# Feed-forward with quantised weights kept as integers and the low-rank term apart

## The chip, the cores and the metric

One core of a Trainium2 chip runs the kernel. The metric is the device time of one execution in microseconds. The engines are TensorE (PE in the rows; its weight loads are PEld), VectorE (DVE), ScalarE (ACT), GpSimd (POOL) and SyncE (SP), each with its own queue that is worked off in order. A semaphore is counted up by one engine and waited for by another.

## The reference, cut to what matters

Two layers act on 16 x 256 rows of 256 numbers, each with an attention half and a feed-forward half. The change touches the feed-forward of the first layer, whose weights are rounded to 8 bits and have a low-rank addition:

```python
def fake_quant_weight(w, bits=BITS):
    qmax = 2.0 ** (bits - 1) - 1
    scale = jnp.max(jnp.abs(w)) / qmax
    wq = jnp.clip(jnp.round(w / scale), -qmax - 1, qmax) * scale
...
def qat_lora_linear(x, W, b, A, B):
    base = jnp.einsum('bsi,oi->bso', x, Wq) + b
    lora = jnp.einsum('bsr,or->bso', jnp.einsum('bsi,ri->bsr', x, A), B)
    return base + SCALING * lora
h = qat_lora_linear(hidden_states, W_fc, b_fc, A_fc, B_fc)
h = jax.nn.gelu(h, approximate=False)
h = qat_lora_linear(h, W_proj, b_proj, A_proj, B_proj)
...
x = x + jnp.tanh(g_ffn[0]) * _L0_ffn_ref(_layernorm(x, axis=-1), ...)
```

The rank is 16, SCALING is 2, W_fc is 1024 x 256 and W_proj is 256 x 1024.

## The kernel before

The kernel runs in stages, one after the other, with a barrier of all engines between them: the gates of the first attention (`mlstm_gates`, 0 to about 76 us), its heads (`mlstm_heads`, to 218), the feed-forward (`phase_lora_ffn`, to 414), the second attention (to about 790) and the routed experts with the shared ones (to the end).

Products in float32 of full precision are made of three passes of TensorE. Each operand is split into a part rounded to the fast format (hi) and a rest (lo), and `three_passes` (lines 29 to 34) adds hi x hi, hi x lo and lo x hi in PSUM.

**The gate stage.** Eight steps n each take 512 rows: DVE makes the statistics and the normalised rows `z`, PE turns them (`turn`), ACT copies them, and PE makes the gate rows (`context_part`, `query_part`). Between these steps the two weights of the feed-forward are prepared. PE multiplies the low-rank factors in 8 pieces (`delta_piece`, ahead of everything else on its queue) and ACT keeps each piece times 2 (`keep_delta`). DVE takes the largest absolute value (`largest`); PE turns the maxima of the partitions (`turn_amax`, which stands behind the pieces), DVE derives the step (`scales`), rounds (`quantise`) and adds the low-rank product (`add_delta`); ACT makes the hi part (`split_w1`, `split_w2`) and DVE the lo part (`low_part`).

**The feed-forward.** Eight chunks n each take 512 rows (T = 4 tiles of 128). The hidden layer has KF = 8 blocks m of 128 units by 512 rows, in HR = 4 PSUM banks `hid`. For each block PE issues 2 x 3 products of 512 columns. ACT then runs the gelu twice, once in float32 (`g_full`, of which there are GR = 2) and once rounded (`g_hi`), and DVE subtracts (`g_lo`). PE's `outputs(n)` makes 4 tiles x 8 blocks x 3 products of 256 columns into `y`, and it may start with the blocks below EARLY = 6. Between `hidden(n)` and `outputs(n)` PE turns the next chunk's rows (`transpose_z(n + 1)`) into two banks `zt`, which ACT and DVE split. DVE adds `y` to `x_all` (`add_x`), in two halves. The order of work on each engine is written by hand: on PE hidden, transpose, outputs; on DVE statistics and norm of the next chunk, the eight `g_lo`, the split of `zt`, `add_x`. POOL takes the power for the norm and adds the output bias.

The quoted lines are the order on PE before.

```python
            with pe.Fori(0, CHUNKS - 1) as n:
                hidden(n)
                transpose_z(n + 1)
                outputs(n)
            hidden(CHUNKS - 1)
            outputs(CHUNKS - 1)
```

## Time and profile before

| | us |
|---|---|
| median of 3 runs | 1389.59 |
| lowest, highest | 1383.13, 1390.19 |
| span of the profiled execution | 1389.1 |
| feed-forward, PE's first product to the last addition | 220.0 to 414.4 |

The profile is one execution. A page gives the busy time of each engine; further views list the instructions in order of time, the groups of instructions, the waits, and the busy time in chosen stretches. PE's products overlap: a product of 512 columns is listed with 0.40 us, while the next starts 0.233 us behind it, so its cost is the distance of starts. The granted clock of PE is given as a share of 2.4 GHz; it is 1.00 or 0.50.

### The profile page before, as it was taken

How to read it: one execution, taken by the hardware profiler on the slowest of the kernel's cores; microseconds unless marked ns; L12 is line 12 of the kernel's file. 1: busy time of each engine (PE TensorE's matmuls, PEld its weight loads, DVE VectorE, ACT ScalarE, POOL GpSimd, SP SyncE). 2: the span in 40 equal slices, each digit the busy share in tenths (PEclk: the TensorE clock that was granted, in tenths of full speed). 3: DMA queues.
4: the chain of work that ended last, by engine and by line, in shares of the span. 5: the costliest groups of instructions: out<-in, count | busy, mean ns of one | idle time of the engine just before them, and what ended most of it. 6: DMA issues, size and time to landing. Idle time of an engine off the chain costs nothing. (4 is left out here: it accounts for less than half of the span.)

```text
span 1389.1 us, 28714 instructions
## 1 busy us (share of the span) xinstructions
PE 1214.8 (87%) x9632; PEld 1021.2 (74%) x9633; DVE 875.0 (63%) x1963; ACT 713.7 (51%) x1580; POOL 425.8 (31%) x557
## 2 busy tenths in 40 slices
PE   7878887999995899999998689767899999995888
PEld 3246556989884566666666488667899999995888
DVE  4959996454535677777787266335566676662546
ACT  2478874464531466666666443124555555553343
POOL 1148876231302011111110016453033233214552
PEclk9979999999996799999999868788999999997999
DMA  8156531000006243344331056444345555534552
GB/s 287 53 206 201 198 115 46 0 0 0 0 0 109 65 99 98 79 97 100 80 87 48 13 203 217 155 170 164 123 160 165 168 161 172 164 117 171 186 190 76
DMA packets 97630, 164.71 MB, mean 119 GB/s; under 512 B 12263, under 2 KB 71835, under 8 KB 95227
## 3 DMA queue, kind: packets, MB, share of 16 engines
q1 hardware_dynamic: 87643, 136.11, 32.3%
q0 software_dynamic: 9264, 27.01, 5.9%
q8 instruction: 57, 0.93, 0.3%
q10 hardware_dynamic: 624, 0.32, 0.1%
q14 instruction: 42, 0.34, 0.1%
HBM read 103.66 MB, written 33.69 MB: 99 GB/s over the span
## 5 line engine op out<-in xcount | busy, mean ns | idle before, releaser
L1449 DVE TENSOR_REDUCE c_mx<-c_s 128x2 f32<-128x512 f32 x256 | 164.5, 685 | 73.1 <-PE c_s L1591 73.1
L1372 ACT ACTIVATE c_probs<-c_t 128x512 f32<-128x512 f32 x256 | 138.9, 595 | 8.8 <-PE c_t L1613 6.0
L2405 ACT ACTIVATE de_g_full<-de_hid,d_e_bias 128x256 f32<-128x256 f32 x156 | 77.1, 494 | 105.5 <-PE de_hid L34 105.5
L32 PE MATMUL de_hid<-de_zt_hi,d_e_hi 128*128 128x256 f32 x312 | 90.5, 290 | 1.4 <-DVE de_zt_lo L2429 1.4
L957 ACT ACTIVATE b_g_full<-b_hid,b_b 128x512 f32<-128x512 f32 x64 | 44.2, 691 | 90.1 <-PE b_hid L34 71.3
L1591 PE MATMUL c_s<-c_kt,c_qt 48*128 48x256 f32 x512 | 64.8, 332 | 26.9 <-DVE c_mx L1449 26.9
L34 PE MATMUL de_y_ps<-d_w_hi,de_g_lo 128*128 x312 | 88.2, 283 | 0.0
L32 PE MATMUL de_y_ps<-d_w_hi,de_g_hi 128*128 x312 | 88.1, 282 | 0.0
L33 PE MATMUL de_y_ps<-d_w_lo,de_g_hi 128*128 x312 | 88.0, 282 | 0.0
L34 PE MATMUL de_hid<-de_zt_hi,d_e_lo 128*128 128x256 f32 x312 | 87.1, 279 | 0.0
L33 PE MATMUL de_hid<-de_zt_lo,d_e_hi 128*128 128x256 f32 x312 | 87.1, 279 | 0.0
L1310 POOL CAST c_ct_hi<-c_c_raw 128x512 fp32r<-128x512 f32 x15 | 9.1, 609 | 243.6 <-PE c_misc L34 243.6
L2562 POOL DMA_INDIRECT dc_rows<-d_y_rows,d_pos x64 | 61.8, 966 | 69.0 <-DVE x_all L2595 32.6
L2434 DVE TENSOR_TENSOR de_g_lo<-de_g_full,de_g_hi 128x256 fp32r<-128x256 f32 x156 | 64.7, 454 | 26.5 <-ACT de_g_hi L2406 26.5
L2406 ACT ACTIVATE de_g_hi<-de_hid,d_e_bias 128x256 fp32r<-128x256 f32 x156 | 77.9, 499 | 0.0
L1591 PEld LDWEIGHTS c_s<-c_kt,c_qt 48*128 48x128 f32 x512 | 41.3, 197 | 43.9 <-DVE c_mx L1449 25.0
L32 PE MATMUL b_y<-b_w_hi,b_g_hi 128*128 128x256 f32 x256 | 72.9, 285 | 0.7 <-DVE b_g_lo L1048 0.7
L33 PE MATMUL b_y<-b_w_lo,b_g_hi 128*128 128x256 f32 x256 | 72.4, 283 | 0.0
L34 PE MATMUL b_y<-b_w_hi,b_g_lo 128*128 128x256 f32 x256 | 72.4, 283 | 0.0
L1625 PE MATMUL c_o<-c_probs,c_va 128*32 128x256 f32 x1024 | 70.7, 395 | 1.2 <-ACT c_probs L1372 1.2
L1951 POOL DMA_INDIRECT d_z_rows<-dr_z,dr_pos_i x56 | 55.6, 994 | 50.1 <-DVE dr_pos_i L2099 34.2
L1613 PEld LDWEIGHTS c_t<-c_qt,c_kt 50*128 50x128 f32 x512 | 39.8, 191 | 41.7 <-issue 24.5
(385 smaller groups left out, 4159.4 us busy)
## 6 DMA issues: line engine op xcount, KB each, us to landing
d_e_raw<-in_w SPq DMA_DIRECT2D x39, 514.0 KB, 5.4
a_mb<-a_maxima SPq DMA_DIRECT2D x16, 1024.0 KB, 7.3
d_z_in<-d_z_rows POOLq DMA_DIRECT2D x39, 256.0 KB, 3.9
d_y_rows<-de_ys SPq DMA_DIRECT2D x39, 256.0 KB
c_kt<-c_k_hi SPq DMA_DIRECT2D x64, 128.0 KB, 3.1
c_qt<-c_q_hi SPq DMA_DIRECT2D x64, 128.0 KB, 3.3
d_zt_kept<-d_w_hi SPq DMA_DIRECT2D x32, 256.0 KB
d_w_hi<-d_zt_kept SPq DMA_DIRECT2D x16, 512.0 KB, 3.7
```

The lines of the kernel that those rows point to most:

```text
L32: tensor.matmul(out, lhs_hi, rhs_hi, start=start, stop=False)
L33: tensor.matmul(out, lhs_hi, rhs_lo, start=False, stop=False)
L34: return tensor.matmul(out, lhs_lo, rhs_hi, start=False, stop=stop)
L1372: act.activation(probs[h % PR][:], t_ps[k][:], ACT.Exp).then_inc(exp_done, 1)
L1449: dve.tensor_reduce(mx[n % 2][:, :, k, p:p + 1], s_ps[h % SB][:], AX.X, ALU.max).then_inc(max_done, 1)
L1591: mm = pe.matmul(s_ps[(first + k) % SB][:, j, :], qt[u][rows, p, j * P:(j + 1) * P], kt[u][rows, p, :], start=True, stop=True)
L1625: mm = pe.matmul(o_ps[OSLOT * i:OSLOT * (i + 1), g % 2, :], va[n % R][:, j, h, :], probs[(n * H + h) % PR][:, j, :], start=(j == 0), stop= ...
L1951: pool.indirect_dma_start(z_rows, bass.IndirectOffsetOnAxis(ap=pos_i[:, at:at + 1], axis=0), z_tile(i), None).then_inc(scattered[2 * i // ...
L2405: act.activation(g_full[:, m, :], hid[m][:, 0:TOK], ACT.Gelu, bias=bias[u][:, m:m + 1]).then_inc(gelu_full, 1)
L2406: act.activation(g_hi[u][:, m, :], hid[m][:, 0:TOK], ACT.Gelu, bias=bias[u][:, m:m + 1]).then_inc(gelu_hi, 1)
L2434: dve.tensor_tensor(g_lo[u][:, m, :], g_full[:, m, :], g_hi[u][:, m, :], ALU.subtract).then_inc(gelu_lo, 1)
L2562: pool.indirect_dma_start(rows[n % RR][:, t * TOP + k, :], None, y_rows, bass.IndirectOffsetOnAxis(ap=M.pos[:, T * n + t, k:k + 1], axis=0 ...
```

## The change

The quantised weight is a step size times an integer of at most 8 bits. After the change the weights `w1` and `w2` hold the integers themselves, which the fast format holds whole, so their lo part is zero and is left out: a product of weight and activation takes two passes (hi and lo of the activation). The step size is applied after the sum: as ACT's `scale` in the gelu (a tensor, one value per partition) and as DVE's scalar in `add_x`.

The low-rank term is no longer multiplied out. For the first layer PE lowers the rows to the rank with `down` (`lower(n)`, 4 products of 512 columns), ACT rounds the result into `low`, DVE puts the lo part beside it, and one further product per block (`raised(m)`) adds the term to `hid`. For the second layer `w2` is 32 columns wider (288), so that `outputs` also gives the lowered rows; DVE copies them (`keep_low2`), PE turns them (`turn_low2`), ACT rounds, DVE makes the lo part (`split_low2`), and 4 products of 256 columns add the term to `y` (`close`). These last steps of chunk n stand inside `hidden(n + 1)`. The up factors are divided by the step size in the gate stage (`raise_hi`, `raise_lo`).

PSUM is dealt out anew: HR = 3 banks `hid`, one bank `turned` for both halves of `zt` and both lowered results, four banks `y`. EARLY is 5. In the gate stage `delta_piece`, `keep_delta`, both `add_delta` and the four splits of the weights are gone, and two new loads (`lora_down`, `lora_up`, 0.57 MB) take the place of four (0.16 MB).

```diff
+        self.G = 2 * rank
+        self.WIDE = self.D + self.G
+        self.w1, self.w2 = sb("w1", [P, self.KD, self.FF]), sb("w2", [P, self.KF, self.WIDE])
+        self.down, self.up = sb("down", [P, self.KD, P]), sb("up", [P, self.FF + self.D])
...
-            act.wait_ge(tanh_done, 1)
-            act.activation(tanh_2[:], tanh_g[:, 2:3], ACT.Copy, scale=2.0).then_inc(tanh_done, 1)
-
-            def keep_delta(k):
-                i, q = divmod(k, PIECES)
-                act.wait_ge(delta_done, k + 1)
-                if k == PIECES:
-                    act.wait_ge(tanh_done, 2)
-                act.activation(delta[i][:, PIECE * q:PIECE * (q + 1)], delta_ps[k % 2], ACT.Identity,
-                               scale=2.0 if i == 0 else tanh_2[:]).then_inc(delta_kept, 1)
...
+            def raise_hi(i):
+                cols = slice(0, lora.FF) if i == 0 else slice(lora.FF, lora.FF + D)
+                act.wait_ge(inverted, i + 1)
+                act.activation(lora.up[0:3 * G, cols], up_raw[:, cols], ACT.Identity, scale=inv2[0:3 * G, i:i + 1]).then_inc(up_hi_done, 1)
...
             def quantise(i):
                 flat = w_raw[i][:]
+                kept = lora.w1[:].rearrange("p a b -> p (a b)") if i == 0 else lora.w2[:, :, 0:D]
                 chained(dve.tensor_scalar(flat, flat, inv[:, i:i + 1], ROUND, ALU.mult, ALU.add))
                 chained(dve.tensor_scalar(flat, flat, -ROUND, QMAX, ALU.add, ALU.min))
-                chained(dve.tensor_scalar(flat, flat, -QMAX - 1.0, scale[:, i:i + 1], ALU.max, ALU.mult))
-
-            def add_delta():
-                flat = w_raw[0][:]
-                dve.wait_ge(delta_kept, PIECES)
...
-            def delta_piece(k):
-                i, q = divmod(k, PIECES)
-                after(pe, delta_kept, k - 1)
...
-                pe.wait_ge(delta_kept, 2 * PIECES)
...
-    HR = 4
+    HR = 3
     GR = 2
-    EARLY = 6
+    EARLY = 5
...
+            def round_low2(n):
+                act.wait_ge(low2_turned, n + 1)
+                act.activation(low2[:], turned[:], ACT.Copy).then_inc(low2_hi_done, 1)
+
+            def gelu(n, m):
+                act.wait_ge(hid_done, n * KF + m + 1)
+                act.wait_ge(gelu_lo, n * KF + m + 1)
+                act.activation(g_full[:, m % GR, :], hid[m % HR][:], ACT.Gelu,
+                               bias=b1[:, m:m + 1], scale=lora.scale[:, 0:1]).then_inc(gelu_full, 1)
+                act.activation(g_hi[:, m, :], hid[m % HR][:], ACT.Gelu,
+                               bias=b1[:, m:m + 1], scale=lora.scale[:, 0:1]).then_inc(gelu_hi, 1)
+
+            round_low(0)
+            for m in range(KF):
+                gelu(0, m)
+            with act.Fori(0, CHUNKS - 1) as n:
+                split_zt(n + 1)
+                round_low(n + 1)
                 for m in range(KF):
-                    act.wait_ge(hid_done, n * KF + m + 1)
-                    act.wait_ge(gelu_lo, n * KF + m + 1)
-                    act.activation(g_full[:, m % GR, :], hid[m % HR][:], ACT.Gelu,
-                                   bias=b1[:, m:m + 1]).then_inc(gelu_full, 1)
-                    act.activation(g_hi[:, m, :], hid[m % HR][:], ACT.Gelu,
-                                   bias=b1[:, m:m + 1]).then_inc(gelu_hi, 1)
-
-            with act.Fori(0, CHUNKS - 1) as n:
-                gelus(n)
-                split_zt(n + 1)
-            gelus(CHUNKS - 1)
+                    gelu(n + 1, m)
+                    if m == 2:
+                        round_low2(n)
...
+            def split_low(n):
+                dve.wait_ge(low_hi_done, n + 1)
+                dve.tensor_tensor(low[pair, :], turned[pair, :], low[pair, :], ALU.subtract).then_inc(low_lo_done, 1)
+
+            def keep_low2(n):
+                for t in range(T):
+                    dve.wait_ge(sums_done, n * T + t + 1)
+                    dve.tensor_copy(low2_rows[:, t, 0:3 * G].rearrange("p (k g) -> p k g", k=3),
+                                    y[t][:, D:WIDE].rearrange("p (k g) -> p k g", k=1).broadcast_to([P, 3, G])).then_inc(low2_kept, 1)
+
+            def split_low2(n):
+                dve.wait_ge(low2_hi_done, n + 1)
+                dve.tensor_tensor(low2[pair, :], turned[pair, :], low2[pair, :], ALU.subtract).then_inc(low2_lo_done, 1)
+
+            def split_gelu(n, m):
+                dve.wait_ge(gelu_hi, n * KF + m + 1)
+                dve.wait_ge(gelu_full, n * KF + m + 1)
+                dve.tensor_tensor(g_lo[:, m, :], g_full[:, m % GR, :], g_hi[:, m, :],
+                                  ALU.subtract).then_inc(gelu_lo, 1)
+
+            def add_x(n, t):
+                dve.wait_ge(y_done, n * T + t + 1)
+                dve.wait_ge(x_biased, n * T + T)
+                xs = x_all[:, n * T + t, :]
+                dve.scalar_tensor_tensor(out=xs, in0=y[t][:, 0:D], scalar=lora.scale[:, 1:2], in1=xs,
+                                         op0=ALU.mult, op1=ALU.add).then_inc(x_added, 1)
...
+            def between(n, more):
                 split_zt(n + 1)
-                add_x(n)
-
+                if more:
+                    stat(n + 2)
+                else:
+                    dve.wait_ge(w_loaded, 64)
+                    dve.tensor_scalar(w_raw[:, :, 3 * D:], w_raw[:, :, 3 * D:], tanh_g[:, 1:2], None, ALU.mult).then_inc(wc_scaled, 1)
+                split_low(n + 1)
+                keep_low2(n)
+                if more:
+                    norm(n + 2)
+                for m in range(KF):
+                    split_gelu(n + 1, m)
+                    if m == 3:
+                        split_low2(n)
+                    if m >= T:
+                        add_x(n, m - T)
...
+            def lower(n):
+                pe.wait_ge(zt_lo_done, n * KD + KD)
                 for c in range(KD):
-                    for t in range(T):
-                        mm = pe.transpose(zt[c][:, t * P:(t + 1) * P], z[:, t, c * P:(c + 1) * P], ident[:])
-                    mm.then_inc(zt_done, 1)
-
-            def hidden(n):
-                pe.wait_ge(zt_lo_done, n * KD + KD)
+                    for part in (zt_hi, zt_lo):
+                        mm = pe.matmul(turned[:], down[:, c, :], part[:, c, :], start=(c == 0 and part is zt_hi), stop=(c == KD - 1 and part is zt_lo))
+                mm.then_inc(low_done, 1)
+
+            def base(n, m):
+                if m >= HR:
+                    pe.wait_ge(gelu_hi, n * KF + m + 1 - HR)
+                for c in range(KD):
+                    for part in (zt_hi, zt_lo):
+                        pe.matmul(hid[m % HR][:], w1[:, c, m * P:(m + 1) * P], part[:, c, :], start=(c == 0 and part is zt_hi), stop=False)
+
+            def raised(m):
+                pe.matmul(hid[m % HR][:], up[:, m * P:(m + 1) * P], low[:], start=False, stop=True).then_inc(hid_done, 1)
...
+            def hidden(n, tail):
                 for m in range(KF):
-                    pe.wait_ge(gelu_hi, n * KF + m + 1)
-                    cols = slice(m * P, (m + 1) * P)
-                    for c in range(KD):
-                        mm = three_passes(pe, hid[m % HR][:], (w1_hi[:, c, cols], w1_lo[:, c, cols]),
-                                          (zt_hi[:, c, :], zt_lo[:, c, :]), c == 0, c == KD - 1)
-                    mm.then_inc(hid_done, 1)
-
-            def outputs(n):
-                def product(t, m):
-                    cols = slice(t * P, (t + 1) * P)
-                    return three_passes(pe, y[t // 2][:, t % 2, :], (g_hi[:, m, cols], g_lo[:, m, cols]),
-                                        (w2_hi[:, m, :], w2_lo[:, m, :]), m == 0, m == KF - 1)
-
-
-                pe.wait_ge(x_added, n * (T // 2))
+                    base(n, m)
+                    if m == 0:
+                        pe.wait_ge(low_lo_done, n + 1)
+                    raised(m)
+                    if tail and m == 1:
+                        turn_low2(n - 1)
+                    if tail and m == 3:
+                        close(n - 1)
...
+            def product(t, m):
+                cols = slice(t * P, (t + 1) * P)
+                pe.matmul(y[t][:, 0:WIDE], g_hi[:, m, cols], w2[:, m, :], start=(m == 0), stop=False)
+                return pe.matmul(y[t][:, 0:WIDE], g_lo[:, m, cols], w2[:, m, :], start=False, stop=(m == KF - 1))
...
+            def outputs(n, more):
+                if more:
+                    transpose_z(n + 1, 0)
                 pe.wait_ge(gelu_lo, GR + n * KF + EARLY)
-                for t in range(0, T, 2):
+                for t in range(T):
                     for m in range(EARLY):
                         product(t, m)
+                if more:
+                    transpose_z(n + 1, 1)
                 pe.wait_ge(gelu_lo, GR + n * KF + KF)
                 for t in range(T):
-                    for m in range(0 if t % 2 else EARLY, KF):
+                    for m in range(EARLY, KF):
                         mm = product(t, m)
-                    if t % 2:
-                        mm.then_inc(y_done, 1)
-
+                    mm.then_inc(sums_done, 1)
+                    if more and t == 1:
+                        lower(n + 1)
...
+            def turn_low2(n):
+                pe.wait_ge(low2_kept, n * T + T)
+                for t in range(T):
+                    mm = pe.transpose(turned[:, t * P:(t + 1) * P], low2_rows[:, t, :], ident[:])
+                mm.then_inc(low2_turned, 1)
+
+            def close(n):
+                pe.wait_ge(low2_lo_done, n + 1)
+                for t in range(T):
+                    pe.matmul(y[t][:, 0:D], low2[:, t * P:(t + 1) * P], up[:, FF:FF + D], start=False, stop=True,
+                              skip_group_check=True).then_inc(y_done, 1)
+
+            lower(0)
+            hidden_first()
             with pe.Fori(0, CHUNKS - 1) as n:
-                hidden(n)
-                transpose_z(n + 1)
-                outputs(n)
-            hidden(CHUNKS - 1)
-            outputs(CHUNKS - 1)
+                outputs(n, True)
+                hidden(n + 1, True)
+                pe.wait_ge(x_added, n * T + T)
```

On PE, where block 3 of the hidden layer ends and block 4 begins, before (the names in brackets are semaphores, whose names are used again from an earlier stage; here the one that counts rounded gelus):

```order
L34 MATMUL b_hid3<-b_zt_hi,b_w1_lo 128x512
L32 MATMUL b_hid3<-b_zt_hi,b_w1_hi 128x512
L33 MATMUL b_hid3<-b_zt_lo,b_w1_hi 128x512
L34 MATMUL b_hid3<-b_zt_hi,b_w1_lo 128x512
L1127 REGISTER_ALU
L32 MATMUL b_hid0<-b_zt_hi,b_w1_hi 128x512 [waits ag_ready]
```

The same place after, inside the loop (`ag_x_loaded5` counts DVE's `split_low2`, `ag_kt_loaded0` the rounded gelus):

```order
L1151 MATMUL b_hid0<-b_zt_lo,b_w1 128x512
L1154 MATMUL b_hid0<-b_low,b_up 128x512
L1208 MATMUL b_y0<-b_up,b_low2 128x256 [waits ag_x_loaded5]
L1208 MATMUL b_y1<-b_up,b_low2 128x256
L1208 MATMUL b_y2<-b_up,b_low2 128x256
L1208 MATMUL b_y3<-b_up,b_low2 128x256
L1148 REGISTER_ALU
L1151 MATMUL b_hid1<-b_zt_hi,b_w1 128x512 [waits ag_kt_loaded0]
```

The closing products of the chunk before stand between the two blocks, and the first of them waits for DVE.

On DVE at that place after (blocks 2 to 4 of the gelu; `ag_x_loaded4` counts ACT's rounding of `low2`, the other two the gelus):

```order
L1048 TENSOR_TENSOR b_g_lo<-b_g_full,b_g_hi 128x512 [waits ag_x_loaded7,ag_kt_loaded0]
L1046 REGISTER_ALU
L1048 TENSOR_TENSOR b_g_lo<-b_g_full,b_g_hi 128x512 [waits ag_x_loaded7,ag_kt_loaded0]
L1043 TENSOR_TENSOR b_low2<-b_turned,b_low2 32x512 [waits ag_x_loaded4]
L1046 REGISTER_ALU
L1048 TENSOR_TENSOR b_g_lo<-b_g_full,b_g_hi 128x512 [waits ag_x_loaded7,ag_kt_loaded0]
L1055 ISA [waits ag_w_loaded0,ag_kt_loaded2]
L1055 SCALAR_TENSOR_TENSOR x_all<-b_y0,b_scale,x_all 128x256
```

`split_low2` stands behind the low part of gelu 3, and the first addition to `x_all` behind that of gelu 4; before, eight low parts stood in a row there and the additions behind them and the split of `zt`.

On PE at the end of the loop's body after (`ag_kt_loaded3` counts the additions to `x_all`):

```order
L1151 MATMUL b_hid1<-b_zt_lo,b_w1 128x512
L1154 MATMUL b_hid1<-b_low,b_up 128x512
L1213 REGISTER_ALU [waits ag_kt_loaded3]
L1213 COMPARE_AND_BRANCH
L1179 MATMUL b_y0<-b_w2,b_g_hi 128x288 [waits ag_kt_loaded1]
```

Before, the wait for the additions stood at the head of `outputs`, behind the hidden layer, and was for the additions of the chunk before; now a wait for those of the chunk that the body began with stands behind the next chunk's hidden layer.

## Rows read from the trace of the kernel before

**Rows 1.** The page: span, and busy time, share and instructions of the engines.
```profile
span 1389.1 us, 28714 instructions
PE 1214.8 (87%) x9632; PEld 1021.2 (74%) x9633; DVE 875.0 (63%) x1963; ACT 713.7 (51%) x1580; POOL 425.8 (31%) x557
```

**Rows 2.** Busy time by stretch, one in the feed-forward; last PEclk, DMA share, GB/s.
```profile
265.00:290.00 25.00, 25.00 (x165) 22.72 (x165) 11.72 (x24) 11.94 (x19) 5.87 (x6) 1.00 0.00 0
```

**Rows 3.** Waits of PE from 237 to 413.9: total us, times, longest.
```profile
PE b_y L32 <- DVE b_g_lo L1048: 0.7, 1, 0.7
```

**Rows 4.** Groups of instructions, 205 to 415: busy us, mean ns, idle before.
```profile
L1048 DVE TENSOR_TENSOR b_g_lo<-b_g_full,b_g_hi 128x512 fp32r<-128x512 f32 x64 | 49.6, 785 | 23.3 <-ACT b_g_hi L959 23.2
...
L957 ACT ACTIVATE b_g_full<-b_hid,b_b 128x512 f32<-128x512 f32 x64 | 44.2, 691 | 90.1 <-PE b_hid L34 71.3 <-DVE b_g_lo L1048 16.9
L959 ACT ACTIVATE b_g_hi<-b_hid,b_b 128x512 fp32r<-128x512 f32 x64 | 44.0, 687 | 0.0
```

**Rows 5.** PE in order of time, one chunk: start us, length us, instruction.
```profile
249.04 0.40 PE L32 MATMUL b_hid<-b_zt_hi,b_w_hi 128*128 128x512 f32 x1
...
260.24 1.03 PE L1121 MATMUL b_zt<-ident,b_z 128*128 128x128 f32 x8
261.03 0.36 PE L32 MATMUL b_y<-b_w_hi,b_g_hi 128*128 128x256 f32 x1
...
272.63 0.40 PE L32 MATMUL b_hid<-b_zt_hi,b_w_hi 128*128 128x512 f32 x1
```

**Rows 6.** PE, ACT and DVE in order of time, last block of the last chunk.
```profile
401.80 0.39 PE L34 MATMUL b_hid<-b_zt_hi,b_w_lo 128*128 128x512 f32 x1
...
402.23 0.69 ACT L957 ACTIVATE b_g_full<-b_hid,b_b 128x512 f32<-128x512 f32 x1
402.82 0.68 ACT L959 ACTIVATE b_g_hi<-b_hid,b_b 128x512 fp32r<-128x512 f32 x1
...
403.53 0.69 DVE L1048 TENSOR_TENSOR b_g_lo<-b_g_full,b_g_hi 128x512 fp32r<-128x512 f32 x1 [0.71 <-ACT b_g_hi L959]
```

**Rows 7.** PE and DVE in order of time, start and end of the stage.
```profile
220.04 0.79 PE L32 MATMUL b_hid<-b_zt_hi,b_w_hi 128*128 128x512 f32 x1 [4.27 <-DVEq L1062]
...
237.46 0.35 PE L32 MATMUL b_y<-b_w_hi,b_g_hi 128*128 128x256 f32 x1 [0.66 <-DVE b_g_lo L1048]
...
229.46 1.38 DVE L1036 TENSOR_SCALAR b_z<-x_all,b_mean_var,b_rstd 128x256 f32<-128x256 f32 x4 [3.20 <-POOL b_rstd L978]
...
413.75 0.69 DVE L1056 TENSOR_TENSOR x_all<-x_all,b_y 128x512 f32<-128x512 f32 x1 [2.91 <-PE b_y L34]
```

**Rows 8.** PE after three idle times, and stretches behind them as in rows 2.
```profile
36.97 1.11 PE L519 MATMUL ag_tz<-ident,ag_z 128*128 128x128 f32 x8 [3.59 <-DVE ag_z L402]
...
232.85 0.50 PE L32 MATMUL b_hid<-b_zt_hi,b_w_hi 128*128 128x512 f32 x1 [1.61 <-ACT b_g_hi L959]
...
416.23 0.66 PE L1549 MATMUL c_misc<-ident,c_z 128*128 128x128 f32 x4 [2.52 <-DVEq L1492]
...
416.80:420.20 3.40, 3.40 (x18) 3.40 (x18) 0.81 (x2) 1.20 (x2) 1.80 (x3) 0.50 0.18 29
...
38.00:41.30 3.30, 3.30 (x5) 0.78 (x5) 3.16 (x11) 0.75 (x2) 0.23 (x1) 0.50 0.00 0
...
230.50:236.00 5.50, 3.89 (x19) 2.81 (x18) 4.35 (x7) 4.46 (x8) 5.08 (x5) 1.00 0.00 0
```

**Rows 9.** PE, DVE and ACT in order of time, gate stage.
```profile
18.46 1.91 PE L509 MATMUL ag_tok<-ag_factors 16*128 16x256 f32 x4
...
13.37 1.41 DVE L390 BATCH_NORM_STATS2 ag_stats<-x_all 128x6 f32<-128x256 f32 x4 [5.16 <-DMA x_all<-in_x]
...
28.99 0.29 DVE L413 TENSOR_REDUCE ag_amax<-ag_spare 128x1 f32<-128x128 f32 x1 [6.70 <-PE ag_spare L526]
...
14.17 0.60 ACT L334 ACTIVATE ag_delta<-ag_tok 128x512 f32<-128x512 f32 x1 [1.11 <-PE ag_tok L506]
15.29 0.69 ACT L334 ACTIVATE b_delta<-ag_spare,ag_tanh 128x512 f32<-128x512 f32 x1 [0.52 <-PE ag_spare L509]
```

More of the change, by code:

```diff
@@ L934, in phase_lora_ffn @@
         block = ctx.enter_context(nc.Block())
+        pair = slice(G, 2 * G)
         @block.sync
@@ L945, in _ @@
         def _(act):
-            act.sem_inc(gelu_hi, HR)
             def split_zt(n):
@@ L1051, in add_x @@
[L1051 to L1062 removed]
+                    dve.tensor_tensor(zt_lo[:, c, :], turned[:], zt_hi[:, c, :], ALU.subtract).then_inc(zt_lo_done, 1)
@@ L1086, in _ @@
             norm(1)
-            split_gelu(0)
-            split_zt(1)
-            add_x(0)
+            for m in range(KF):
+                split_gelu(0, m)
             dve.wait_ge(h_x_done, HT)
-            with dve.Fori(1, CHUNKS - 1) as n:
-                step(n)
-            dve.wait_ge(w_loaded, 64)
-            dve.tensor_scalar(w_raw[:, :, 3 * D:], w_raw[:, :, 3 * D:], tanh_g[:, 1:2], None, ALU.mult).then_inc(wc_scaled, 1)
-            split_gelu(CHUNKS - 1)
-            dve.wait_ge(x_added, T // 2)
+            dve.wait_ge(padded, 1)
+            with dve.Fori(0, CHUNKS - 2) as n:
+                between(n, True)
+            between(CHUNKS - 2, False)
+            dve.wait_ge(x_added, T)
             for j in range(attn.J):
@@ L1162 @@
+            outputs(CHUNKS - 1, False)
+            turn_low2(CHUNKS - 1)
+            close(CHUNKS - 1)
 class RoutedRows:
```

213 lines of the change are left out of this document (101 added, 112 removed).

## Prediction

> **What bounds the kernel now.** I read the page first: TensorE (PE) is busy for 87% of the span [rows 1]. The change touches two of five stages: the gate stage (0 to 76 us) and the feed-forward (220 to 414 us). So next the busy time by stretch: in a 25 us stretch of the feed-forward PE is busy for all of it at full granted clock, ScalarE (ACT) and VectorE (DVE) for half [rows 2]. Then the waits of PE alone: from 237 us to the end of the stage it waits once, 0.7 us [rows 3]. The feed-forward is bound by PE's issue rate, and the other two have slack. The reader is to see that this slack is an average: within a chunk each gelu pair (1.15 us of ACT per 512-column block) hangs on PE's last product and DVE's low part hangs on the gelu [rows 4, 6].
>
> **Part 1, work taken off PE.** One chunk before: 48 products of 512 columns in 249.04 to 260.24 (11.20 us, 0.2333 each), 8 transposes in 0.79 (0.099 each), 96 products of 256 columns in 11.60 (0.1208 each), together 23.59 us [rows 5]. After, a chunk has 40 products of 512 columns for the hidden layer and 4 for the lowered rank (44 x 0.2333 = 10.27), 64 of 288 columns, 12 transposes (1.19) and 4 closing products of 256 columns (0.48). No row shows 288 columns; it lies between 0.1208 and 0.2333. I take the straight line between the two, 0.135, since it is nearest to 256 columns: 8.63. Sum 20.57, so 3.0 us less per chunk. At 0.1208 the saving would be 3.9, at 0.2333 a loss of 3.3. The Trainium skill ("TensorE: Matmul & The Clock Gate", section "Back-to-back issue gap") gives N/2.4 + 2.5 ns for one product, 122.5 ns at 288 columns; as an estimate by that page the chunk would be 0.8 us shorter still, 6 us over eight chunks, but its 215.8 ns at 512 columns is below the 233 ns of rows 5, so the trace decides.
>
> **Part 2, two new waits, which PE has nothing to cover with.** Before, PE waits in the hidden layer only for a bank that was read four blocks ago, and between chunks only for sums that were added long before. After, the second layer's low-rank term is closed inside the next chunk's hidden layer.
>
> Wait A: behind block 3 PE issues `close`, which needs DVE's low part of `low2`. On DVE that instruction stands behind the low part of gelu 3, and gelu 3 needs the block that PE has just issued. So PE waits for the whole ladder PE, ACT, ACT, DVE, DVE. Rows 6 show this ladder at the end of a chunk: the block's last product starts at 401.80, the gelus at 402.23 and 402.82, DVE's low part ends at 403.53 + 0.69 = 404.22. From PE's next free slot (402.03) that is 2.19 us. To it come DVE's `low2` part, 0.65 more (a 512-column subtraction of the same kind), and 0.53 because ACT rounds `low2` just ahead of gelu 3: 3.4 us. Behind the waiting instruction on PE are `close` and blocks 4 to 7, and ACT and DVE wait for these.
>
> Wait B: at the loop's end PE waits for `x_added`. The fourth `add_x` stands on DVE behind the low part of gelu 7, so the same ladder runs again: 2.19 + about 0.4 for a 256-column add = 2.6 us. Behind it are the next chunk's transposes and all its output products, though those need only gelus 0 to 4.
>
> Each wait also costs 0.1 for the restart (the product after the gap at 232.85 takes 0.50 [rows 8], others 0.40). Together 6.2 us per chunk in seven chunks, against 3.0 saved: a period of 23.59 becomes 26.7. The range of A is 2.2 (its ACT and DVE parts hidden) to 4; of B 2.2 to 3.
>
> **Part 3, the two ends of the stage.** First chunk: PE starts at 220.04 [rows 7]. Now 4 lowering products come first, at half clock as before at this place (the first one takes 0.79 [rows 7] and not 0.40 [rows 5]; spaced by 0.45), and DVE's first instruction waits for ACT's rounding of them: 1.8 + 0.6 + 0.7 + 0.2 = 3.3 us before its statistics start. These lead to the normalised rows at 229.46, behind which the first gelu low part stands; it goes to 232.8. ACT then needs three gelu pairs more for the five blocks, and PE's output products begin near 239.1 (before 237.46). With 8.6 of products, 0.4 of transposes and 0.9 of lowering, the second chunk starts at 249.1, as before (249.04 [rows 5]). So the first chunk gains nothing. Periods 1 to 6: 6 x 3.15 = +18.9. Last chunk: before, from 390.6 (249.04 + 6 x 23.59) to 414.44 [rows 7], 23.9 us. After: hidden layer 9.3 + 0.9 of turning and closing + 6.2 of waits + 8.6 of products = 25.0, then a tail that nothing covers (copy, 4 transposes, ACT's rounding 0.6, DVE's part 0.7, closing, four adds): about 4.3. Sum 29.3, +5.4. Stage: +24.3 us.
>
> **Part 4, the clock.** A PE idle of 2.52 us is followed by a stretch at 0.50 of the granted clock (1.2 GHz in place of 2.4) from 416.8 to 420.2; one of 3.59 us by one from 38 to 41.3; one of 1.61 us leaves it at 1.00 [rows 8]. The new waits are 3.4 and 2.6 us, so most should be followed by such a stretch. It halves 3.4 us of work, which PE must then make up: 1.7 us, in stretches that PE bounds (blocks 4 to 7 after A, output products after B). Fourteen waits give 0 to 24 us; since B stands at the edge of what rows 8 show, I count ten: +17. The Trainium skill ("TensorE: Matmul & The Clock Gate", section "Loop structure matters more than you think") says the same of a loop whose every pass waits between bursts, namely that each burst then runs cold; rows 8 bear that out for single gaps, and no run here shows it for a loop.
>
> **Part 5, the gate stage.** Sixteen groups of small products and their ACT copies go, and so do DVE's two sums and two low parts. PE was at them until 20.4 us, which kept the turned maxima from DVE: it sat idle 6.70 us until 28.99 [rows 9]. Then came PE's idle of 3.59 us until 36.97 [rows 8], and from there PE is the chain to the stage's end. After, DVE's second statistics start at 13.37 [rows 9] plus about 1 us, since the new factor table adds 0.4 MB to what loads then. Statistics, normalising and maxima put the first turn on PE near 18, and with two half-clock groups behind it the maxima near 24.5; DVE goes on near 24.8 in place of 28.99, and the third turn falls near 32.6, not 36.97: -4 us, an estimate from these rows. DVE's work at the stage's end gets shorter too, but there the last rows' placing is later, so that is hidden. Bounds: -8 (all of DVE's gain) to 0 (a further cold stretch).
>
> **Part 6, a second per-partition operand in the gelu.** ACT's copy with a tensor as scale took 0.69, with a number 0.60 [rows 9]. The gelu already has a tensor bias at 0.69 [rows 4]. If a second tensor costs again, every ladder grows by up to 0.3: 0 to 5 us, taken as 2.
>
> **The sum.** 24.3 + 17 - 4 + 2 = +39 us on the profiled execution's 1389.1, hence 1428. The median of the three runs is 1389.6, 0.5 from it, so no correction. Attention and the experts are untouched.
>
> **Rivals.** (1) The waits come but the clock stays up: gaps of 2.6 and 3.4 us inside dense work need not behave like those of rows 8. Then 1389 + 24 - 4 + 0 to 2 = 1409 to 1411. For it: the gap of 1.61 us. Against: that of 2.52. 15 in 100.
> (2) Faster: the two waits are covered. The place is PE's queue behind block 3 and block 7. It decides at 3.0 us of wait per chunk; below it the change wins. If ACT and DVE ran ahead so that both vanish, 7 x 3.0 and the gate stage's 4 give 1364. Against it: the ladder of rows 6 has 2.19 us in it twice, whatever the order of the rest, and the program leaves PE no other instruction there. 5 in 100; another 3 for a balance within 7 us.
> (3) Worse: every wait is followed by a cold stretch, and cold PE also stretches the ladders (a block takes 2.1 us in place of 1.2), with dearer gelus: 24 + 24 + 5 and some lengthening, 1440 to 1460. 9 in 100.
> (4) 288-column products at 0.2333: +6.3 per chunk, 50 us more. Nothing speaks for it but a form that no row shows; 2 in 100.
>
> **How the numbers follow.** The forecast has 66 in 100. A measurement of this kernel can tell about 0.5% (7 us) from no change. Slower by more: 66 + 15 + 9 + 2 = 92; within it 3; faster 5. The range must hold rival 1 with its lower bound (-8 in the gate stage, 1405) and the upper bounds of clock and gelu (1442): 1403 to 1446.
>
> **What would show each step.** In the profile of after: PE waits seven times about 3.4 us ahead of the closing products and seven times about 2.6 us ahead of the transposes at the loop's head; a period of 27 to 30 us; granted clock at 0.50 after most of them; 288-column products 0.135 apart; the stage 220 to 414 us grown to about 235 us; the end of the gate stage 4 us earlier. I am wrong if PE's waits in the stage sum to less than 20 us, or if the clock stays at 1.00 throughout (then 1410).

## The result, and the profile after

The changed kernel takes 1447.5 us (1437.2 to 1450.1) beside 1387.1 (1383.1 to 1390.2) of the kernel before, run on the same chip: 1.041 of it, with an interval of 1.036 to 1.046. On the 1389.6 us that the prediction started from, the ratio gives 1446.8 (1440 to 1454). Slower was right. The size was not: 1428 was forecast, and the time lies at the upper bound of the range (1446), 0.8 us past it.

The page after. The first line is the span, the second busy time, share and instructions of the engines, as in [rows 1]:
```profile
span 1445.6 us, 28329 instructions
PE 1202.7 (83%) x9384; PEld 1009.0 (70%) x9385; DVE 890.2 (62%) x2034; ACT 719.4 (50%) x1579; POOL 420.9 (29%) x559
```
PE is busy 12 us less than in [rows 1] and the span is 56.5 us longer. Work was taken away, and idle time came in its place. The waits of PE between 205 and 470 us say where (total us, times, longest); this is the counterpart of [rows 3], which had one of 0.7:
```profile
PE b_y L1208 <- DVE b_low L1043: 26.9, 8, 3.6
PE b_turned L1136 <- DVE x_all L1055: 20.7, 6, 3.6
PE b_hid L1151 <- ACT b_g_hi L938: 7.4, 2, 6.3
PE b_turned L1143 <- DVEq L1093: 4.4, 1, 4.4
PE b_y L1179 <- DVE x_all L1055: 3.4, 1, 3.4
```
The first line is wait A, `close` behind block 3 (seven of 3.6 and, at the stage's end, one of 1.4). The second and the fifth are wait B at the loop's end, seven times 3.3 to 3.6. (The profile leaves buffer numbers out: `b_low` at L1043 is `low2`.) The third stands in the first chunk, where the kernel before had one of 1.6 [rows 8]. The fourth was there before [rows 7].

One period of the loop, the stretch from one chunk's output products to the next one's, beside the 23.59 us of [rows 5]. The columns are those of [rows 2]:
```profile
328.55:359.84 31.29, 24.17 (x125) 21.03 (x125) 14.60 (x32) 13.39 (x20) 4.98 (x6) 0.89 0.00 0
```
The two waits inside it, PE in order of time:
```profile
349.43 0.74 PE L1208 MATMUL b_y<-b_up,b_low 128*128 128x256 f32 x4 [3.64 <-DVE b_low L1043]
...
359.84 0.65 PE L1136 MATMUL b_turned<-ident,b_z 128*128 128x128 f32 x4 [3.48 <-DVE x_all L1055]
```
31.29 = 24.17 busy + 3.64 + 3.48, to the last digit. The other whole periods take 30.8 to 32.2. The granted clock is 0.89 over the period, where [rows 2] had 1.00, so part of the 24.17 is work at half clock.

The ladder behind wait A in another chunk, PE, ACT and DVE in order of time, which answers to [rows 6]:
```profile
251.02 0.39 PE L1154 MATMUL b_hid<-b_low,b_up 128*128 128x512 f32 x1
251.63 0.59 ACT L931 ACTIVATE b_low<-b_turned 128x512 fp32r<-128x512 f32 x1
...
252.10 0.78 ACT L936 ACTIVATE b_g_full<-b_hid,b_b,b_scale 128x512 f32<-128x512 f32 x1
252.77 0.79 ACT L938 ACTIVATE b_g_hi<-b_hid,b_b,b_scale 128x512 fp32r<-128x512 f32 x1
253.59 0.69 DVE L1048 TENSOR_TENSOR b_g_lo<-b_g_full,b_g_hi 128x512 fp32r<-128x512 f32 x1 [0.86 <-ACT b_g_hi L938]
254.31 0.68 DVE L1043 TENSOR_TENSOR b_low<-b_turned,b_low 32x512 fp32r<-32x512 f32 x1
255.05 1.22 PE L1208 MATMUL b_y<-b_up,b_low 128*128 128x256 f32 x4 [3.64 <-DVE b_low L1043]
```
It is the ladder that was forecast: block 3, ACT's rounding of `low2`, the gelu pair, DVE's two low parts, `close`. Two things in it are longer than forecast. The gelus take 0.78 in place of the 0.69 of [rows 4], and the pair starts 1.08 us behind the block's last product in place of the 0.43 of [rows 6] and the 0.53 put down for ACT's rounding. The closing products take 1.22 in place of 0.74: they run at half clock.

By stages, each read off the first and last instruction:

| stage | before | after | difference | forecast |
|---|---|---|---|---|
| start to the heads' first product | 78.00 | 74.48 | -3.5 | -4 |
| from there to PE's start in the feed-forward | 142.04 | 139.43 | -2.6 | 0 |
| feed-forward, to the end of its last addition | 194.40 | 253.98 | +59.6 | +43 |
| the rest | 974.7 | 977.7 | +3.0 | 0 |

The sum is the 56.5 us by which the spans differ. The heads' 2.6 us are not put down to the change: their code is untouched, and in the eleven profiled executions of this document they take 138.2 to 142.7 us. The rest is untouched too. The gate stage did what was forecast. The feed-forward is 16 us over.

### The profile page after: what moved, and what is told of

The parts are those of the page before. It is cut to its first block and busy times, and to the rows that moved or that the text cites. A ratio compares the mean times of both kernels' runs of the same rounds, so it can differ in the third digit from the quotient of the medians.

```text
span 1445.6 us, 28329 instructions
## 1 busy us (share of the span) xinstructions
PE 1202.7 (83%) x9384; PEld 1009.0 (70%) x9385; DVE 890.2 (62%) x2034; ACT 719.4 (50%) x1579; POOL 420.9 (29%) x559
## 5 line engine op out<-in xcount | busy, mean ns | idle before, releaser
L1048 DVE TENSOR_TENSOR b_g_lo<-b_g_full,b_g_hi 128x512 fp32r<-128x512 f32 x64 | 50.6, 791 | 63.1 <-ACT b_g_hi L938 62.8
L936 ACT ACTIVATE b_g_full<-b_hid,b_b,b_scale 128x512 f32<-128x512 f32 x64 | 50.0, 781 | 59.0 <-PE b_hid L1154 52.6
L1179 PE MATMUL b_y<-b_w,b_g_hi 128*128 128x288 f32 x256 | 76.5, 322 | 3.4 <-DVE x_all L1055 3.4
L1180 PE MATMUL b_y<-b_w,b_g_lo 128*128 128x288 f32 x256 | 74.6, 315 | 0.0
L1674 PE MATMUL c_t<-c_qt,c_kt 50*128 50x256 f32 x512 | 62.7, 323 | 7.4 <-ACT c_probs L1433 7.2
```

Of the source, the lines that this page charges most:

```text
L1179: pe.matmul(y[t][:, 0:WIDE], g_hi[:, m, cols], w2[:, m, :], start=(m == 0), stop=False)
L1180: return pe.matmul(y[t][:, 0:WIDE], g_lo[:, m, cols], w2[:, m, :], start=False, stop=(m == KF - 1))
L1674: mm = pe.matmul(t_ps[k][:, i, :], kt[u][rows, p, i * P:(i + 1) * P], qt[u][rows, p, :], start=True, stop=True)
```

## The experiments

They were made on several chips. The kernel before took 1379, 1317 and 1389 us there, and its feed-forward stage is unmoved by that (194.4 us in [rows 7]; 194.5 in a kernel of the 1317 us chip whose feed-forward is that of before). So times are compared as ratios to the kernel before on the same chip, and costs are read from the stage.

**1. Wait B taken away.** TensorE's program is untouched; VectorE does the four additions earlier.
```
                 for m in range(KF):
                     split_gelu(n + 1, m)
                     if m == 3:
                         split_low2(n)
-                    if m >= T:
-                        add_x(n, m - T)
+                        for t in range(T):
+                            add_x(n, t)
```


> Only VectorE's queue changes: the four additions of chunk n stand right behind the low part of low2 (ahead of the low parts of gelus 4 to 7), so x_added is complete long before TensorE reaches the loop's end. Theory (each of the two waits costs its length and a stretch at half clock behind it, and nothing else is late): wait B goes, 7 x (3.5 wait + 0.1 restart + 1.7 cold) = 37 us less than the changed kernel's 1447, so 1410; wait A stays at 3.6; seven half-clock stretches in the stage in place of 14; period 31.3 becomes 26. Rival 1 (the cold stretches cost nothing, ScalarE's pace hides them): 25 us less, 1422. Rival 2 (the wait only moves: ScalarE needs 1.32 us for a block and TensorE 1.17, so TensorE meets the late gelus at the output products or in wait A): 0 to 12 us less, 1435 or more.

Measured: 1405.9 us, 1.0195 of the kernel before (1.014 to 1.025), so 0.0217 less than the changed kernel, 30 us (by the two intervals, 20 to 40). The stage, which is the sharper measure, takes 220.9 us in place of 254.0, 33 less, where the theory had 37. Wait B is gone from the list of waits, A is unchanged at 3.64. Three periods of this kernel, columns as in [rows 2]:
```profile
263.12:287.67 24.55, 20.90 (x126) 18.41 (x125) 14.33 (x33) 13.03 (x20) 4.97 (x6) 1.00 0.00 0
287.67:313.73 26.06, 22.42 (x126) 19.53 (x125) 14.65 (x33) 13.45 (x22) 4.97 (x6) 0.93 0.00 0
313.73:340.80 27.07, 23.42 (x126) 20.40 (x125) 14.54 (x33) 13.44 (x21) 4.97 (x6) 0.87 0.00 0
```
Each has 3.65 us of idle, which is wait A. At a granted clock of 1.00 the period is 24.55. At 0.93 it is 1.5 us longer and at 0.87 2.5 us, with the same waits. So a half-clock stretch costs what its work needs extra, and the first period shows that a 3.6 us wait need not be followed by one. The later periods take 27.2, hence 4.1 less than the 31.3 of the changed kernel and not the 5.3 of the theory: the half-clock stretches behind A became longer when those behind B went. (By the distances of the 512-column products, the last four run at half clock for 4.7 to 5.1 us each behind the closing products, in the changed kernel for 1.7 to 3.4.) Rival 2 falls. Rival 1 is not refuted by the time, but by the three periods, which price the cold directly.

**2. Wait A shortened.** Only the places of ACT's rounding and DVE's low part of `low2` in their queues change.
```
                     gelu(n + 1, m)
-                    if m == 2:
+                    if m == 1:
                         round_low2(n)
...
                     split_gelu(n + 1, m)
-                    if m == 3:
+                    if m == 1:
                         split_low2(n)
```


> Only the queues of ScalarE and VectorE change: ScalarE rounds low2 behind gelu 1 and not gelu 2, VectorE takes its low part behind the low part of gelu 1 and not of gelu 3. TensorE's order is untouched. Theory: the closing products stand about 2.7 us behind block 1 on TensorE, and low2 is ready 3.0 us behind it, so wait A shrinks from 3.6 to at most 0.5; the cold stretches behind it go; 7 x (3.2 + 0.1 + 1.7) = 35 us less than 1447, so 1412; B stays at 3.5. Rival 1 (cold stretches cost nothing): 1424. Rival 2 (it is not the place in the queue but ScalarE's lag that makes the wait): A still 1.5 us or more, 1430 or more.

Measured: 1412.2 us, 1.0226 (1.018 to 1.027), 26 us less than the changed kernel; the stage takes 224.2 us, 30 less, where the theory had 35. A falls from 3.64 to 0.95, not to 0.5; B stays. Two waits of this kernel, PE in order of time:
```profile
306.92 0.74 PE L1208 MATMUL b_y<-b_up,b_low 128*128 128x256 f32 x4 [0.95 <-DVE b_low L1043]
315.96 1.11 PE L1136 MATMUL b_turned<-ident,b_z 128*128 128x128 f32 x4 [3.64 <-DVE x_all L1055]
```
and the period that ends with the second of them, at a clock of nearly 1.00 (columns of [rows 2]):
```profile
290.27:315.96 25.69, 21.10 (x124) 18.31 (x125) 14.35 (x32) 13.22 (x20) 4.98 (x6) 0.99 0.00 0
```
25.69 = 21.10 + 0.95 + 3.64. This is the shortest; the others take 27.1 to 27.3, with a half-clock stretch behind B worth 1.5 us. That is 4.1 less than 31.3, of which 2.7 are the wait, so the cold stretch behind A did cost something and rival 1 falls with rival 2. The wait did hang on the place in the queue: 2.7 of its 3.64 us went with two instructions moved. Behind the wait of 0.95 no half-clock stretch stands.

**3. Both.** The additions stand behind the low part of gelu 3, `split_low2` behind that of gelu 1, and ACT rounds `low2` behind gelu 1.

> Both edits of queue order together (the additions behind the low part of gelu 3, so that they do not stand ahead of it). Theory: 72 us less than the changed kernel's 1447, so 1375, that is 0.991 of the kernel before; no wait of TensorE over 1 us in periods 1 to 6; a period of 20.7 to 21.5 us; the clock at 1.00 from the second chunk on. This is what the lighter products are worth alone. Rival (the two savings are not additive, since with one wait gone the other's ladder takes over): 1390 to 1410, a period of 23 to 26.

Measured: 1369.3 us, 0.992 (0.989 to 0.995). A period (columns of [rows 2]):
```profile
283.33:305.18 21.85, 20.90 (x126) 18.42 (x124) 14.16 (x33) 13.09 (x21) 4.98 (x6) 1.00 0.00 0
```
and its only wait, PE in order of time:
```profile
299.93 0.74 PE L1209 MATMUL b_y<-b_up,b_low 128*128 128x256 f32 x4 [0.95 <-DVE b_low L1043]
```
The stage takes 187.9 us, 66 less than in the changed kernel, and the two edits alone gave 33 and 30: the savings add up, and the 3 us more fit a loop that now runs at full clock throughout. The rival falls. The same products as in the changed kernel, with ACT's and DVE's queues in an order that hardly lets PE wait, take 0.8% less than the kernel before. The loss of the change lies in that order.

**4. The clock alone.** The waits stay, and PE is kept busy in them by products whose results are dropped.
```
+            def idle(i, count):
+                for _ in range(count):
+                    pe.matmul(hid[i][:], w1[:, 0, 0:P], zt_hi[:, 0, :], start=True, stop=True)
...
                     if tail and m == 3:
+                        pe.wait_ge(gelu_hi, n * KF + 2)
+                        idle(1, 12)
                         close(n - 1)
...
                 hidden(n + 1, True)
+                pe.wait_ge(gelu_hi, n * KF + KF + 6)
+                idle(2, 11)
                 pe.wait_ge(x_added, n * T + T)
```


> The changed kernel with products added whose results are dropped: 12 products of 512 columns into the bank of block 4 ahead of the closing products, 11 into the bank of block 2 ahead of the wait at the loop's end. The waits stay where they are, but TensorE is busy through most of them. Theory: the clock stays at 1.00 through the stage, TensorE's idle in each falls below 1 us, and the 14 cold stretches go, each worth up to 1.7 us: up to 24 us less than 1447, so 1423 to 1428. Rival (what is cold was hidden by ScalarE and VectorE anyway): within 5 us of 1447, with the clock at 1.00.

Measured: 1416.9 us, 1.0271 (1.022 to 1.033), 20 us less than the changed kernel with 161 products more. The two waits that are left of a period, PE in order of time:
```profile
312.80 0.74 PE L1214 MATMUL b_y<-b_up,b_low 128*128 128x256 f32 x4 [0.84 <-DVE b_low L1043]
321.90 0.65 PE L1136 MATMUL b_turned<-ident,b_z 128*128 128x128 f32 x4 [1.12 <-DVE x_all L1055]
```
The period itself (columns of [rows 2]):
```profile
293.46:321.90 28.44, 26.48 (x148) 22.63 (x148) 14.61 (x32) 13.30 (x20) 4.98 (x6) 1.00 0.00 0
```
The clock is at 1.00, idle is about 1 us at each place, and the period is 28.44 in place of 31.29. So of the 31.3 us, 2.9 are the clock's. The other 28.4 are the 20.9 of work and 7.5 at the two waits, which the added products fill without shortening them. The rival falls.

**5. The changed kernel again,** on the chip of the next three.

> The changed kernel as it is, beside the others of this call. Both theories: 1.041 of the kernel before, stage of the feed-forward 254 us.

Measured: 1374.1 us beside 1316.9, 1.0445 (1.043 to 1.046); the stage takes 254.2 us. The loss is 57 us on a shorter program, as it was 56.5 between the spans above.

**6. The second operand of the gelu,** left out of both gelus of a pair.
```
-                               bias=b1[:, m:m + 1], scale=lora.scale[:, 0:1])
+                               bias=b1[:, m:m + 1])
```


> The changed kernel with the gelus called without the tensor scale (the first layer's step size is left out of the computation); nothing else differs. Theory (the second per-partition operand costs 0.09 us per gelu, a block takes ScalarE 1.32 us and TensorE 1.17, so ScalarE falls behind block by block and both waits are measured from its end): a gelu takes 0.69, a block 1.15; wait A falls from 3.64 to about 3.0, wait B from 3.5 to about 2.7; 7 x 1.5 = 10 us less than the changed kernel. Rival (the waits are set by TensorE's last block and the ladder, not by ScalarE's lag): A and B lose only the last pair's 0.17 each, 2 us.

Measured: 1366.1 us, 1.0379 (1.036 to 1.040), beside 1.0445: 8 us less; the stage takes 245.3 us, 8.9 less. The gelus' group from 246 to 460 us (busy us, mean ns, idle before) in the changed kernel:
```profile
L936 ACT ACTIVATE b_g_full<-b_hid,b_b,b_scale 128x512 f32<-128x512 f32 x56 | 43.8, 781 | 50.4 <-PE b_hid L1154 50.2
```
and in this one:
```profile
L936 ACT ACTIVATE b_g_full<-b_hid,b_b 128x512 f32<-128x512 f32 x56 | 38.7, 690 | 51.3 <-PE b_hid L1154 51.1
```
with its waits, PE in order of time:
```profile
347.56 0.84 PE L1208 MATMUL b_y<-b_up,b_low 128*128 128x256 f32 x4 [3.28 <-DVE b_low L1043]
357.47 0.65 PE L1136 MATMUL b_turned<-ident,b_z 128*128 128x128 f32 x4 [2.94 <-DVE x_all L1055]
```
The operand costs 0.09 us in each gelu. With it a pair keeps ACT for 1.34 us (two starts of gelus lie 0.67 apart, 252.10 and 252.77 in the ladder above), longer than PE's 1.17 for a block, so ACT falls behind wherever blocks follow each other without a pause, and each wait is measured from ACT's last. A was expected at 3.0 and is 3.28, B at 2.7 and is 2.94; the two together are 0.9 us shorter and not 1.5, about 6 us in seven chunks. The rest of the 8.9 us fits the clock: the output products of the last chunk start at 0.60 us each in the changed kernel and at 0.39 in this one, and from there to the stage's end 1.4 us are saved. The theory is right in kind, and near in the sum. The rival's 2 us is too little.

**7. Two more steps on top of 3.**
```
-                    if tail and m == 3:
+                    if tail and m == 4:
                         close(n - 1)
...
+            split_gelu(0, 0)
+            split_gelu(0, 1)
             late_norm()
+            split_gelu(0, 2)
             norm(1)
-            for m in range(KF):
+            for m in range(3, KF):
                 split_gelu(0, m)
```


> The version with both edits of queue order, and two more: the closing products stand behind block 4 and not block 3 (low2 is ready 0.9 us late behind block 3), and in the first chunk VectorE takes the low parts of gelus 0 to 2 ahead of normalising the second chunk's rows (TensorE waits 5.8 us there for gelu 2). Theory: the last wait in the loop goes, a period of 20.9 in place of 21.83, 7 x 0.9 = 6 us; the first chunk's wait goes, 5 to 6 us; so 12 us less than 0.9922 of the kernel before, that is 0.983 to 0.985 of it. Rival (the rows of the second chunk are then normalised late, and TensorE waits for them at the first output products instead): the first chunk gains 0 to 2, ratio 0.987 to 0.989.

Measured: 1297.2 us beside 1316.9, 0.987 (0.985 to 0.989). The period is 20.7, so the first step holds. The second did not. The waits of PE in the first chunk:
```profile
227.57 0.50 PE L1155 MATMUL b_hid<-b_zt_hi,b_w 128*128 128x512 f32 x1 [1.80 <-ACT b_g_hi L938]
239.11 1.12 PE L1140 MATMUL b_turned<-ident,b_z 128*128 128x128 f32 x4 [4.38 <-DVE b_zt_lo L1029]
```
and DVE's instruction that the second one waits for:
```profile
238.36 0.69 DVE L1029 TENSOR_TENSOR b_zt_lo<-b_turned,b_zt_hi 128x512 fp32r<-128x512 f32 x1 [4.94 <-POOL x_all L986]
```
The wait for gelu 2 fell from 5.8 to 1.8 us, and 4.4 us came up behind it: DVE waited ahead of the loop for GpSimd's late update of the last rows. The rival had the size right (0.987) and the mechanism wrong.

**8. That wait moved** to the end of each pass of the loop, since the rows that it guards are read six chunks later.
```
                        for t in range(T):
                            add_x(n, t)
+                if more:
+                    dve.wait_ge(h_x_done, HT)
...
-            dve.wait_ge(h_x_done, HT)
             dve.wait_ge(padded, 1)
```

> The version before this one, with one wait of VectorE moved: the wait for GpSimd's late update of the last rows stood ahead of the loop, and in the first chunk it held the low part of the transposed rows (4.9 us on VectorE, 4.4 us on TensorE). Those rows are read only six chunks later, so the wait now stands at the end of each pass of the loop. Theory: TensorE's 4.4 us wait and the half-clock stretch behind it go; from TensorE's start to the second chunk's output products 38 to 40 us in place of 43.9; the stage 176 to 178 us in place of 181.5; 4 to 6 us less in all, 0.982 to 0.984 of the kernel before. Rival (another late operation of the first chunk takes its place, GpSimd's reciprocal roots or the gelus): under 2 us less, 0.986.

Measured: 1365.0 us beside 1388.6, 0.982 (0.979 to 0.985). From PE's start to the second chunk's output products it is 37.1 us (217.25 to 254.38), and the stage takes 175.0 us, both a little better than expected, and the rival's 0.986 lies outside the interval. PE has no wait from there to the last chunk:
```profile
275.08:295.78 20.70, 20.70 (x126) 18.29 (x125) 14.09 (x34) 13.11 (x20) 4.99 (x6) 1.00 0.00 0
```
PE is busy for all of the period, as in [rows 2], and the period is 2.9 us shorter than 23.59. Part 1 of the prediction is thereby measured apart: it gave 3.0.

**9. The gate stage alone.**
```
-            for k in range(2 * PIECES):
-                keep_delta(k)
...
-                dve.tensor_tensor(flat, flat, delta[0][:], ALU.add).then_inc(summed, 1)
+                dve.sem_inc(summed, 1)
...
-            for k in range(PIECES):
-                delta_piece(k)
```
(and the same for the second weight)

> The kernel before with the low-rank term left out of the weights (the sixteen groups of small products, ScalarE's copies of them and VectorE's two sums; the weights are then the quantised ones alone). Everything behind it, the third pass included, stays. Theory (TensorE's small products held back the turned maxima, on which VectorE sat until 28.99): the maxima are turned near 24.6, the third turn falls near 33 and not 36.97, the gate stage ends 3.5 to 4 us earlier as in the changed kernel, all the rest as before. Rival (the shorter stage comes from the sums and low parts of VectorE at the stage's end, or from the integers kept): the third turn stays at 37, and the stage ends at most 1 us earlier.

Measured, in a single run: 1306.6 us beside 1316.9. The third turn:
```profile
31.76 1.97 PE L517 MATMUL ag_tz<-ident,ag_z 128*128 128x128 f32 x8 [3.59 <-DVE ag_z L400]
```
It falls at 31.76 and not at the 36.97 of [rows 8], with the same 3.6 us of idle ahead of it. The heads start at 72.54 in place of 78.00. That is 5.5 us earlier, more than the 3.5 to 4 expected, and the changed kernel of experiment 5, with its third turn at 31.87, starts them at 74.50. So the change pays about 2 us back later in the stage. In its trace (DVE, then ACT, in order of time) stand instructions that experiment 9 has not:
```profile
31.73 0.18 DVE L410 CAST b_down<-ag_down_raw 128x48 fp32r<-128x48 f32 x1
...
32.67 0.29 DVE L417 TENSOR_TENSOR b_w<-ag_down_raw,b_w 128x128 fp32r<-128x128 f32 x1
32.88 1.39 DVE L367 BATCH_NORM_STATS2 ag_stats<-x_all 128x6 f32<-128x256 f32 x4
...
58.74 0.49 ACT L336 ACTIVATE b_up<-ag_up_raw,b_inv 96x256 fp32r<-96x256 f32 x1
```
The factors' splitting holds the fourth statistics back by 1.2 us and ACT's rounding the last rows' copy by 0.4. No run moved these, so this last reading is argued and not shown.

## Why the prediction was right in direction and short in size

**Part 1, work taken off PE: right.** The chunk's work was put at 20.57 us; it is 20.70 where nothing waits (experiment 8) and 20.90 with one short wait (experiment 3). The products of 288 columns, PE in order of time in experiment 3:
```profile
287.22 0.29 PE L1180 MATMUL b_y<-b_w,b_g_hi 128*128 128x288 f32 x1
287.35 0.29 PE L1181 MATMUL b_y<-b_w,b_g_lo 128*128 128x288 f32 x1
287.48 0.30 PE L1180 MATMUL b_y<-b_w,b_g_hi 128*128 128x288 f32 x1
```
They stand 0.13 us apart; the straight line gave 0.135, and rival 4 (0.2333) is out. The Trainium skill ("TensorE: Matmul & The Clock Gate", section "Back-to-back issue gap") would have 122.5 ns, an estimate by its formula for a single product, 0.01 us less, and the trace decides.

**Part 2, the waits: right in place and mechanism, low in size.** A was put at 3.4 and is 3.64. B was put at 2.6, range 2.2 to 3, and is 3.3 to 3.65, outside its range. The ladder was copied from [rows 6], where ACT is not behind. How far it is behind in the changed kernel can be read at blocks 2 and 7, PE's last product and the gelu for it:
```profile
249.86 0.39 PE L1154 MATMUL b_hid<-b_low,b_up 128*128 128x512 f32 x1
250.29 0.78 ACT L936 ACTIVATE b_g_full<-b_hid,b_b,b_scale 128x512 f32<-128x512 f32 x1
...
261.54 0.39 PE L1154 MATMUL b_hid<-b_low,b_up 128*128 128x512 f32 x1
262.44 0.80 ACT L936 ACTIVATE b_g_full<-b_hid,b_b,b_scale 128x512 f32<-128x512 f32 x1
```
At block 2 the gelu starts 0.43 us behind, as in [rows 6]: PE's turning of `low2` behind block 1 has let ACT catch up, so only the pairs of gelus 2 and 3 make A longer. At block 7 it starts 0.90 behind, after four pairs in a row. Experiment 6 fits both: without the operand A is 0.36 us shorter and B 0.4 to 0.7. B's last step was also missed. From DVE's last addition to PE's next product:
```profile
264.54 0.48 DVE L1055 SCALAR_TENSOR_TENSOR x_all<-b_y,b_scale,x_all 128x256 f32 x1
265.57 1.11 PE L1136 MATMUL b_turned<-ident,b_z 128*128 128x128 f32 x4 [3.64 <-DVE x_all L1055]
```
That is 0.55 us from the end of the one to the start of the other, where A has 0.06 between 254.99 and 255.05. B's wait stands at the end of the loop's body, ahead of its branch. That this is the reason was not tried.

**Part 6, the gelu's second operand: the mechanism was named, the price was wrong by far.** It was put at 2 us, range 0 to 5, and costs 8 to 9 (experiment 6). The step that failed is the conclusion "every ladder grows by up to 0.3". It allows for the last pair alone. But 1.34 us per pair is more than PE's 1.17 per block, so every pair that PE gives ACT no pause to make up for adds its excess: two of them ahead of A, four ahead of B, and longer waits bring more half clock. The prediction compared ACT's busy share with the span (half) and never its pace with PE's inside the hidden layer. The price itself was to be had: the Trainium skill ("ScalarE: Activation LUTs", section "What ACT_TABLE_LOAD costs") gives about 93 ns for each operand of this kind, and the trace agrees with 0.690 and 0.781. The prediction left open whether a second one costs again.

**Part 4, the clock: right in kind, counted short.** Ten of fourteen waits at 1.7 were to give 17 us. The stage of the kernel kept warm (experiment 4) takes 233.8 us (214.82 to 448.58) beside 254.0: the clock is worth 20. A half-clock stretch stands behind 13 of the 14 waits of the profiled execution, nearly as rival 3 had it (9 in 100). Of the Trainium skill's example of a loop whose passes each wait and then run cold ("TensorE: Matmul & The Clock Gate", section "Loop structure matters more than you think") the trace bears out only a part: the mean clock is 0.89, most of each pass being at 1.00, and experiment 1's first period is at 1.00 throughout with a wait of 3.65 in it.

**Part 3, the two ends: short by 3 us in the first chunk.** The second hidden layer starts 32.2 us behind PE's start (213.91 to 246.16), forecast 29.1. The normalised rows came when forecast, 12.8 us after the start. The step that failed is "PE's output products begin near 239.1", which asked only when the five gelus would be ready. The first chunk in order of time, PE alone:
```profile
230.32 0.80 PE L1151 MATMUL b_hid<-b_zt_hi,b_w 128*128 128x512 f32 x1 [6.32 <-ACT b_g_hi L938]
...
235.78 0.60 PE L1136 MATMUL b_turned<-ident,b_z 128*128 128x128 f32 x4
...
246.16 0.39 PE L1151 MATMUL b_hid<-b_zt_hi,b_w 128*128 128x512 f32 x1
```
With three banks for the hidden layer in place of four, PE stood before block 5 until gelu 2 was out, and then had blocks 5 to 7 to do, most of it at half clock, before any output product: 5.5 us. This is read from the order of the program and the trace; no run tried four banks.

**Part 5, the gate stage: right in size, in part by luck,** -3.5 against -4. The step itself came as forecast, the third turn at 31.87 (32.6 was put down). But the stage's -3.5 is the balance of -5.5 and +2 (experiment 9), of which the prediction had only the first, and that at -4.

**The sum.** A period was put at 26.7, with 17/7 for the clock and 2/7 for the gelus at 29.4; it is 31.3. Seven times 1.9 is 13 us, the first chunk 3: these are the 16 us by which the stage exceeds its forecast of 43. Of the 1.9, 0.4 are the clock's (2.9 in experiment 4 against 17/7). The others are there at full clock too: in experiment 4 the waits with their restarts take 7.5 against 6.2, the work 20.9 against 20.6, and 0.3 of this had been set down for the gelus. Rival 3, every wait cold with longer ladders and dearer gelus, 1440 to 1460, describes what happened. It had been held apart from Part 6, though dearer gelus make longer ladders, and longer ladders make colder waits: the three terms grow together.

**The faster rival** was not what the change did, but experiment 8 shows that it was within reach without changing any product. The prediction held that "the ladder has 2.19 us in it twice, whatever the order of the rest". That is so only as long as what closes the sum stands behind gelu 3 and gelu 7 in the queues of ACT and DVE. `low2` and the additions need neither gelu. Moved ahead of them, with `close` one block later, they leave PE nothing to wait for.

## What to carry to other kernels

When a step is put between two halves of a bound engine's work, look at what stands ahead of its inputs in the other engines' queues: an operand that is ready early but queued behind a late one is late. Compare paces inside the stretch (1.34 us per pair against 1.17 per block), not busy shares of the span, since an engine that is half idle over the stage can still be the slower one for four blocks in a row. And price waits, clock and the length of the waited-for chain as one case, because they rise together.

## What was not expected of the hardware

- The same wait of PE, 3.64 us at the same place of the program, was followed by no half-clock stretch, by one worth 1.5 us or by one worth 2.5 (experiment 1: clock 1.00, 0.93, 0.87 over the period). Waits of 0.95 us were followed by none.
- An ACT instruction on 128x512 takes 0.60 us with numbers as scale and bias, 0.69 with one tensor of one value per partition and 0.78 with two ([rows 9], [rows 4, 9], and experiment 6's first group).
- At the loop's end PE went on 0.55 us after the addition that it waited for, inside the body 0.06 us after the low part.
